# A decoder layer in a three-deep software pipeline: the recurrence of a batch beside the whole next iteration, its feed-forward one iteration later

## The chip, the core and the metric

The kernel runs on one core of one Trainium2 chip. The metric is the device time of one execution in microseconds. All work is inside one launch; the host only lays out the inputs.

## What is computed

Sixteen independent batches of 256 tokens with 512 channels go through one decoder layer: causal self-attention with 16 heads of 32 channels, a recurrence over the tokens that takes the first result as keys and a second input as values, and an attention that has one shared key and value head, chosen for each token by a gate. Each of the three is added to its input and normalised over the channels.

```python
def _wkv(time_decay, time_first, k, v):       # per channel, over 256 tokens
    w, u = -jnp.exp(time_decay), time_first
    def step(carry, kv_t):
        aa, bb, pp = carry
        kt, vt = kv_t
        ww = u + kt
        q = jnp.maximum(pp, ww)
        e1, e2 = jnp.exp(pp - q), jnp.exp(ww - q)
        y_t = (e1 * aa + e2 * vt) / (e1 * bb + e2)
        ...
...
x = _layernorm(x + _L0_attn_ref(x, Wq, bq, Wk, bk, Wv, bv, Wo, bo))
x = _layernorm(x + _L0_xattn_ref(16, 256, 512, time_decay, time_first, x, ctx_2048))
x = _layernorm(x + _L0_ffn_ref(x, W_gate, W_qkv))
```

The feed-forward (`_L0_ffn_ref`) projects x to q, k and v, keeps for each token the k and v of the head that the gate ranks first, and attends causally with all 16 query heads over these.

## The kernel before

**The work of a batch.** Matrix products are made in three passes of a high and a low part (lines 485 to 487). A is the self-attention: six projections (`project_a`, jobs PA_Q, PA_K, PA_V, two each), four groups of four heads, and two output projections (PA_WO). A group has three tiles of scores for the maxima (`scores_sq`, `sq_a`), whose row maxima VectorE takes (`maxima_a`, line 1368); `max_a` turns them (line 547), ScalarE and VectorE split them into high and low rows (`row_hi`, `rows`), and SyncE copies the two rows under the query stack in SBUF (line 332). Only then come the three tiles of scores in the other orientation (`scores_sk`, `sk_a`, lines 563 to 573), their exponentials on ScalarE (line 1031), `values`, a copy, `turn`, and `normalise` on VectorE. F is the feed-forward with the same four groups (`sq_f`, `sk_f`, `values_f`, `turn_f`, `third_residual`), its projections PF_Q, PF_K, PF_V, the gate (`gate_logits`, `gate_transpose`, `gating`), and the choice of key and value (`pick_key`, `pick_value`), after which `key_transpose` (line 733) turns the key.

**The recurrence** is done per block of 128 channels (c = 0 to 3), two blocks at a time. TensorE turns x1 so that channels lie on partitions (`x1_transpose`, line 620, half 0 and half 1, in PSUM bank pw). VectorE runs a scan and a difference (`recurrence_start`, lines 1422 and 1426), ScalarE five passes (`carry_exps`) and one more (`now_exps`), VectorE two scans (`sums`, lines 1437 and 1439), GpSimd the products around them (`weighted`, `products`, `quotient`), VectorE a reciprocal of 256 columns (`divide`, line 1445). TensorE turns the result back (`y_transpose`, line 645), VectorE adds it (`second_residual`), takes statistics (`second_stats`) and normalises (`second_norm`, line 1410). Then `x2_transpose` (line 620 again) feeds the feed-forward, whose q is split by `fq_hi` on ScalarE and `fq_lo` on VectorE (line 1483).

**The order.** Each engine runs one hand-written list of instructions and waits on semaphores; nothing is reordered. `iteration(t)` of TensorE interleaves A of batch t with F of batch b = t - 1, and in its second part projects q, k and v of batch t + 1. The recurrence of batch t starts in that second part (blocks 0 and 1 first, then 2 and 3) and ends in the first part of iteration t + 1: `y_transpose` 0 inside the projection PA_V + 1, `y_transpose` 1 behind `max_a(t, 1)`, `x2_transpose` six groups of instructions later. SyncE's list holds, in this order, the copies of the k stack, two loads of ctx, more of the k and q stacks and then the rows of maxima. Batch 15's recurrence uses a second set of buffers (`far`), and runs beside the second half of F of batch 14; F of batch 15 runs alone at the end. `keep` issues products whose result is not used.

**Memory.** Two buffers hold x (`x_even`, `x_odd`). `w_key` and `w_e1` lie over the last quarter of `k_stack`, so GpSimd puts back two rows of ones after each recurrence (`ones_back`). `picked` lies in `w_val`.

```python
                project_a(t, PA_V + 1, {1: lambda: y_transpose(b, 0), 2: scores})
                sk_a(t, 0, 2)
                max_a(t, 1)
                y_transpose(b, 1)
                ...
                x2_transpose(b, x_by_parity[1 - odd])
```

## Time and profile before

| | |
|---|---|
| median of 3 runs | 1566.29 us (1560.98 to 1566.89) |
| the profiled execution, its own time | 1569.24 us |
| span of its instructions | 1567.4 us |
| TensorE busy | 1419.3 us, 91% |
| VectorE busy | 1124.4 us, 72% |
| ScalarE busy | 640.0 us, 41% |
| GpSimd busy | 412.3 us, 26% |
| iteration 1 | 101 to 202 us |
| iterations 2 to 15 start about every 93 us | 202 to 1415 us |
| ending | about 1477 to 1567 us |

Read the timeline by the last columns: a row with "[1.05 <-DVE neg_max L1368]" is an instruction before which its engine sat idle for 1.05 us, until line 1368 on VectorE released it. A row without brackets followed the one before it. The engines' busy shares are sums over stages; which wait counts is seen at the place where TensorE stands.

### The profile page before, as it was taken

Reading aid. Unit: us, or ns where it says so; the run is one execution under the profiler, and the core shown is the slowest. Engines: PE = TensorE matmul, PEld = TensorE weight load, DVE = VectorE, ACT = ScalarE, POOL = GpSimd, SP = SyncE. Lnnn points to the kernel's source line nnn. Section 1 sums busy time; section 2 is a strip of 40 time slices with the busy share of each in tenths; the row PEclk is TensorE's granted clock in tenths of the full one; section 3 lists DMA queues with packets and bytes.
Section 4 is the critical chain, followed back from the end, with each engine's and each line's share of the span. In section 5 each row is a group of like instructions: output and inputs, shape, how many; then the busy total and the mean of one; then the engine's idle time right before and its main releaser. Section 6 shows DMA issues by size and latency. Waiting matters only on the chain.

```text
span 1567.4 us, 26626 instructions
## 1 busy us (share of the span) xinstructions
PE 1419.3 (91%) x9941; PEld 1123.7 (72%) x9941; DVE 1124.4 (72%) x2260; ACT 640.0 (41%) x1459; POOL 412.3 (26%) x550
## 2 busy tenths in 40 slices
PE   7879999899998989999899999989999998999886
PEld 6667777677777777777777777777777777777564
DVE  4475777868677686776868677786867768677774
ACT  3442533434344253433435344353434425353322
POOL 1350321414122141321414122141412214032130
PEclk9989999999999999999999999999999999999998
DMA  6432232333213233232333313233321323323110
GB/s 192 133 89 68 55 76 57 88 89 79 79 42 82 75 88 89 59 88 52 71 88 79 92 47 74 65 88 89 79 79 42 82 75 89 88 61 80 32 50 20
DMA packets 63199, 119.50 MB, mean 76 GB/s; under 512 B 14304, under 2 KB 32736, under 8 KB 63072
## 3 DMA queue, kind: packets, MB, share of 16 engines
q1 hardware_dynamic: 60400, 112.56, 28.6%
q10 hardware_dynamic: 2672, 5.24, 1.0%
q8 instruction: 80, 1.31, 0.4%
q14 instruction: 47, 0.39, 0.1%
HBM read 32.81 MB, written 8.39 MB: 26 GB/s over the span
## 4 chain that ended last, share of the span: by engine, by line
PE 59%; DVE 26%; ACT 7%; DMA 3%; issue 3%; SPq 1%; POOL 1%; DVEq 0%; ACTq 0%; POOLq 0%
PE pp L485 8%; PE pp L487 7%; PE pp L486 7%; PE po L590 7%; DVE neg_max L1368 5%; DVE w_key L1445 3%; PE po L594 3%; PE sq L531 3%; DVE w_max L1439 2%; PE sq L525 2%; PE pw L485 2%; PE pw L487 2%; PE pw L486 2%; PE sq L510 2%; DMA q_stack<-max_rows 2%
## 5 line engine op out<-in xcount | busy, mean ns | idle before, releaser
L1031 ACT ACTIVATE prob<-sk 128x512 f32<-128x512 f32 x384 | 215.0, 594 | 464.2 <-PE sk L510 463.7
L1368 DVE TENSOR_REDUCE neg_max<-sq 128x2 f32<-128x512 f32 (+1 forms) x384 | 249.7, 677 | 58.0 <-PE sq L510 54.9
L485 PE MATMUL pp<-xt_hi,w_hi 128*128 128x256 f32 x728 | 220.4, 303 | 20.8 <-DVE w_lo L1355 7.3
L487 PE MATMUL pp<-xt_hi,w_lo 128*128 128x256 f32 x728 | 206.3, 283 | 0.0
L486 PE MATMUL pp<-xt_lo,w_hi 128*128 128x256 f32 x728 | 206.3, 283 | 0.0
L485 PEld LDWEIGHTS pp<-xt_hi,w_hi 128*128 128x128 f32 x728 | 139.8, 192 | 32.9 <-issue 11.8
L486 PEld LDWEIGHTS pp<-xt_lo,w_hi 128*128 128x128 f32 x728 | 139.9, 192 | 0.7
L487 PEld LDWEIGHTS pp<-xt_hi,w_lo 128*128 128x128 f32 x728 | 139.6, 192 | 0.0
L1042 ACT ACTIVATE o_ch<-po 128x512 f32<-128x512 f32 x128 | 75.8, 592 | 136.2 <-PE po L594 136.2
L510 PE MATMUL sq<-mask_qk,ident_b 128*128 128x256 bf16 (+1 forms) x384 | 124.7, 325 | 0.0
L485 PE MATMUL pp<-w_hi,xt_hi 128*128 128x512 f32 x252 | 114.2, 453 | 10.7 <-DVE k_lo L1477 10.7
L510 PE MATMUL sk<-mask_kq,ident_b 128*128 128x256 bf16 (+1 forms) x384 | 123.4, 321 | 0.0
L1854 POOL TENSOR_TENSOR w_ev<-w_e,w_val 128x256 f32<-128x256 f32 x62 | 43.6, 704 | 260.8 <-ACT w_e L1089 229.0
L1445 DVE RECIPROCAL w_key<-w_key 128x256 f32<-128x256 f32 x62 | 107.5, 1734 | 0.0
L1820 POOL TENSOR_TENSOR var_eps<-meanvar,eps 128x2 f32<-128x2 f32 x48 | 9.3, 194 | 359.6 <-DVE meanvar L1404 359.6
L487 PE MATMUL pp<-w_hi,xt_lo 128*128 128x512 f32 x252 | 99.6, 395 | 0.0
L486 PE MATMUL pp<-w_lo,xt_hi 128*128 128x512 f32 x252 | 98.9, 392 | 0.0
L563 PE MATMUL sk<-q_stack,kf_stack 98*128 98x512 f32 x192 | 82.1, 467 | 6.9 <-DMA q_stack<-max_rows 3.3
L1373 DVE TENSOR_TENSOR max_rows<-pt,max_rows 8x128 fp32r<-8x128 f32 x128 | 35.3, 276 | 72.5 <-ACT max_rows L1064 70.0
L1839 POOL TENSOR_TENSOR xt_lo<-x_raw,xt_hi 128x1024 fp32r<-128x1024 f32 x15 | 35.6, 2373 | 189.9 <-ACT xt_hi L1102 189.9
L590 PE MATMUL po<-prob,v_f 128*33 128x256 f32 x512 | 80.0, 388 | 3.5 <-ACT prob L1031 2.3
L590 PE MATMUL po<-prob,v_a 128*33 128x256 f32 x512 | 80.7, 393 | 1.1 <-ACT prob L1031 1.1
(237 smaller groups left out, 3537.1 us busy)
## 6 DMA issues: line engine op xcount, KB each, us to landing
q_stack<-q_hi SPq DMA_DIRECT2D x256, 128.0 KB, 2.4
q_stack<-q_lo SPq DMA_DIRECT2D x128, 128.0 KB, 2.4
k_stack<-k_hi SPq DMA_DIRECT2D x128, 128.0 KB, 2.3
x_raw<-in_xT SPq DMA_DIRECT2D x16, 512.0 KB, 3.8
k_stack<-k_lo SPq DMA_DIRECT2D x64, 128.0 KB, 2.3
w_val<-in_ctxT SPq DMA_DIRECT2D x62, 128.0 KB, 2.2
w_raw<-in_weights ACTq DMA_DIRECT2D x4, 1024.0 KB, 6.5
q_stack<-max_rows SPq DMA_DIRECT2D x256, 4.0 KB
```

The source lines that it names most:

```text
L485: T.matmul(out, lh, rh, start=(c == 0), stop=False, skip_group_check=True)
L486: T.matmul(out, lh, rl, start=False, stop=False, skip_group_check=True)
L487: mm = T.matmul(out, ll, rh, start=False, stop=(c == CC - 1), skip_group_check=True)
L510: return T.matmul(out, ident_b[:], tile[:].unsqueeze(1).to_broadcast([P, heads, P]), start=False, stop=True, skip_group_check=True)
L531: T.matmul(out[:, S * k:S * (k + 1)], q_stack[0:3 * HD, h, P:S], key(h, 0, S, 3 * HD), start=(k == 0), stop=False, skip_group_check=True)
L563: T.matmul(out[:].rearrange("p (h q) -> p h q", h=heads), key(h, lo, P, rows), q_stack[0:rows, h:h + heads, q], start=True, stop=False, sk ...
L590: T.matmul(po[VW * j:VW * j + HD + 1, at:at + S], value(0, HG * g + k), prob0[:, k, :], start=True, stop=False, skip_group_check=True)
L594: mm = T.matmul(po[VW * j:VW * j + HD + 1, at + P:at + S], value(1, HG * g + k), prob1[:, k, :], start=False, stop=True, skip_group_check= ...
L1031: A.activation(dst, sk[n % 2][:], ACT.Exp, scale=SCALE).then_inc(s_exp, 1)
L1042: A.activation(o_ch[:].rearrange("p h q -> p (h q)"), po[:], ACT.Copy).then_inc(s_och, 1)
L1368: V.tensor_reduce(dst, src, AX.X, ALU.max, negate=True).then_inc(s_max, 1)
L1445: V.reciprocal(key, key).then_inc(w_rec, 1)
```

## The change

A third stage is put into the pipeline. `iteration(t)` now works on A of batch t, the recurrence of batch r = t - 1, and F of batch b = t - 2. On TensorE `y_transpose(r, 0)` stands behind `values_a(t, 2)`, `y_transpose(r, 1)` ahead of PA_WO, and `x1_transpose(t, 1)` behind the projection PA_V; the order of groups and projections is the old one. Iteration 1 has no F. The ending holds the rest of F of batch 13, F of batch 14 with the recurrence of batch 15 beside it, and F of batch 15; the `keep`s of the ending and the `far` buffers are gone. x has three buffers; `w_key`, `w_e1`, `k_hi`, `k_lo` and `picked` have memory of their own, and `ones_back` is gone. The recurrence and the feed-forward count their use of bank pw in semaphores of their own (`w_*` and `u_*`).

```diff
-W_JOBS, W_X1J, W_YJ, W_X2J, W_GATE, W_GATE_T = 7, 0, 2, 4, 5, 6
+W_JOBS, W_X1J, W_YJ = 4, 0, 2
+U_JOBS, U_X2, U_GATE, U_GATE_T = 3, 0, 1, 2
 CONSTS = 2
...
-        k_stack, far_max, far_e2, far_d, far_e1, far_key, w_key, w_e1 = overlaid(
...
+        k_stack = sb("k_stack", [P, NH, S], f32r)
+        w_key = sb("w_key", [P, HC, S])
+        w_e1 = sb("w_e1", [P, HC, S])
...
-        x_even = sb("x_even", [P, TT, D])
-        x_odd = sb("x_odd", [P, TT, D])
+        x_bufs = [sb(f"x{i}", [P, TT, D]) for i in range(3)]
...
-        picked = w_val[:].rearrange("p c t -> p (c t)").rearrange("p (h d) -> p h d", h=NH)
+        picked_buf = sb("picked", [P, NH, HD])
+        picked = picked_buf[:]
...
-            def iteration(t, odd, last=False):
-
-
-                b = t - 1
+            def iteration(t, last=False):
+
+
+                r, b = t - 1, t - 2
+                f = b >= 0
...
-                project_a(t, PA_V + 1, {1: lambda: y_transpose(b, 0), 2: scores})
+                project_a(t, PA_V + 1, {2: scores})
                 sk_a(t, 0, 2)
                 max_a(t, 1)
-                y_transpose(b, 1)
...
-                x2_transpose(b, x_by_parity[1 - odd])
+                if f:
+                    x2_transpose(b)
                 out_transpose(t, 0)
                 sq_a(t, 2, 2)
                 values_a(t, 1)
-                project_f(b, PF_Q, lambda: max_a(t, 2))
+                if f:
+                    project_f(b, PF_Q, lambda: max_a(t, 2))
+                else:
+                    max_a(t, 2)
                 turn_a(t, 1)
...
                 sq_a(t, 3, 2)
                 values_a(t, 2)
-                project_f(b, PF_K, lambda: max_a(t, 3))
+                y_transpose(r, 0)
+                if f:
+                    project_f(b, PF_K, lambda: max_a(t, 3))
+                else:
+                    max_a(t, 3)
...
+                    pe.wait_ge(dve_f, F_LINKS * b + F_LINK_PICKED + 1)
+                    values_f(b, 0)
+                    max_f(b, 1, a_free, A_JOBS * a_done)
+                y_transpose(r, 1)
                 project_a(t, PA_WO)
-                turn_f(b, 0)
-                project_a(t, PA_WO + 1, lambda: sk_f(b, 1, 0, 1))
-
-                sq_f(b, 2, 0, 1)
-                sk_f(b, 1, 2)
...
+                project_a(t + 1, PA_V, parts)
+                x1_transpose(t, 1)
+                if f:
+                    max_a(t + 1, 0, f_free, F_JOBS * (b + 1))
+                else:
+                    max_a(t + 1, 0)
                 sq_a(t + 1, 1, 0, 1)
 
...
-                second_residual(b, 0, x_b)
...
                 maxima_a(t, 1, 2)
-                if not (isinstance(t, int) and t < 2):
-                    last_third_residual(t - 2, x_t)
+                if b >= 1:
+                    last_third_residual(b - 1, x_of(b - 1))
                 rows_a(t, 1)
-                second_residual(b, 1, x_b)
-                second_stats(chy, b, x_b)
-                chy.close()
                 normalise_a(cha, t, 0)
-                second_norm(b, x_b)
-
+                if t > 1:
+                    sums(r, 2)
                 maxima_a(t, 2, 0, 1)
...
                 rows_a(t, 2)
-                if not (isinstance(t, int) and t < 2):
-                    third_stats(t - 2, x_t)
+                if t > 1:
+                    sums(r, 3)
+                if b >= 1:
+                    third_stats(b - 1, x_of(b - 1))
                 normalise_a(cha, t, 1)
-                gate_out(b)
-                fq_lo(b, 0)
+                if f:
+                    gate_out(b)
+                if t > 1:
+                    divide(r, 2)
+                if f:
...
+                if t > 1:
+                    divide(r, 3)
+                if f:
...
+                    gating(chf, b)
                 rows_a(t, 3)
-                pick_key(chf, b, 0)
+                second_residual(r, 0, x_r)
+                if f:
+                    pick_key(chf, b, 0)
                 normalise_a(cha, t, 2)
...
                 out_lo(t, 3)
-                rows_f(b, 1)
+                if f:
+                    rows_f(b, 1)
+                second_residual(r, 1, x_r)
                 first_residual(t, 0, x_t)
...
+                if f:
+                    maxima_f(b, 3, 0, 1)
                 sums(t, 0)
+                if f:
+                    maxima_f(b, 3, 2)
+                qk_lo(t + 1, PA_K)
+                if f:
+                    rows_f(b, 3)
                 sums(t, 1)
-                maxima_f(b, 3, 2)
-                qk_lo(t + 1, PA_K)
-                rows_f(b, 3)
+                second_stats(chy, r, x_r)
+                chy.close()
+                qk_lo(t + 1, PA_K + 1)
+                if f:
+                    third_residual(chf, b, 2, x_b)
                 divide(t, 0)
+                second_norm(r, x_r)
+                maxima_a(t + 1, 0, 0, 1)
+                maxima_a(t + 1, 0, 2)
+                rows_a(t + 1, 0)
                 recurrence_start(t, 2)
-                qk_lo(t + 1, PA_K + 1)
-                third_residual(chf, b, 2, x_b)
-
                 recurrence_start(t, 3)
                 divide(t, 1)
-                maxima_a(t + 1, 0, 0, 1)
-                sums(t, 2)
-                maxima_a(t + 1, 0, 2)
-                sums(t, 3)
-                rows_a(t + 1, 0)
-                divide(t, 2)
                 maxima_a(t + 1, 1, 0, 1)
-                divide(t, 3)
...
+                    exps_f(b, 3, 0, 1)
+
+                    exps_f(b, 3, 2)
+                    copy_f(b, 3)
+                    row_hi_a(t + 1, 0, f_mrow[NG - 1], 32 * (b + 1))
+                else:
+                    row_hi_a(t + 1, 0, a_mrow[NG - 1], 32 * (t + 1))
+                value_out(t + 1, 0)
                 carry_exps(t, 2)
                 now_exps(t, 2)
-                copy_f(b, 3)
                 carry_exps(t, 3)
                 now_exps(t, 3)
-                row_hi_a(t + 1, 0, f_mrow[NG - 1], 32 * t)
-                value_out(t + 1, 0)
 
             def x2_split_hi(b):
-                for half, s_job, count, bank in ((0, w_job, W_JOBS * b + W_X2J + 1, pw),
...
+            def iteration(t, last=False):
+                r, b = t - 1, t - 2
+                if t > 1:
+                    weighted(r, 2)
+                    weighted(r, 3)
+                    products(r, 2)
+                    products(r, 3)
+                if b >= 1:
+                    inverse_std(b - 1, 2)
+                    third_bias(b - 1)
+                quotient(r, 2)
+                quotient(r, 3)
+                add_bo(t, x_of(t))
+                if not last:
+                    x_split_lo(t + 1)
+                if t == 1:
                     split_lo(W_FV)
-                if prev and not (isinstance(t, int) and t < 2):
-                    inverse_std(t - 2, 2)
-                    third_bias(t - 2)
-                add_bo(t, x_by_parity[odd])
-                x_split_lo(t + 1)
-                if not prev:
-                    split_lo(W_FQ)
                 inverse_std(t, 0)
-                if not prev:
-                    split_lo(W_FK)
+                if last:
+                    inverse_std(r, 1)
+                    return
                 weighted(t, 0)
                 weighted(t, 1)
...
-                b = LAST - 1
+                b = LAST - 2
                 sq_f(b, 2, 2)
-                x1_transpose(LAST, 0, x_by_parity[LAST % 2])
+                x1_transpose(LAST, 0)
+                values_f(b, 1)
                 max_f(b, 2)
-                x1_transpose(LAST, 1, x_by_parity[LAST % 2])
-                values_f(b, 1)
+                x2_transpose(LAST - 1)
                 turn_f(b, 1)
                 sk_f(b, 2, 0, 1)
                 sq_f(b, 3, 0, 1)
-                pe.wait_ge(w_free, W_JOBS * LAST + W_YJ)
-                keep(pw, 9)
+                project_f(LAST - 1, PF_Q)
                 sk_f(b, 2, 2)
-                keep(pw, 10)
                 sq_f(b, 3, 2)
-                keep(pw, 20)
+                values_f(b, 2)
                 max_f(b, 3)
-                values_f(b, 2)
+                project_f(LAST - 1, PF_Q + 1)
                 turn_f(b, 2)
                 sk_f(b, 3, 0, 1)
+                x1_transpose(LAST, 1)
                 sk_f(b, 3, 2)
+                values_f(b, 3)
+                b = LAST - 1
+                gate_logits(b)
+                project_f(b, PF_K)
+                gate_transpose(b)
+                turn_f(b - 1, 3)
+                project_f(b, PF_K + 1)
+                project_f(b, PF_V)
+                key_transpose(b, f_free, F_JOBS * b)
                 y_transpose(LAST, 0)
+                pe.wait_ge(f_free, F_JOBS * b + F_KT + 1)
+                pe.wait_ge(f_max, TILES * b)
+                sq_f(b, 0, 0, 1, 2)
+                project_f(b, PF_V + 1)
+                max_f(b, 0)
+                sq_f(b, 1, 0, 1, 2)
+                pe.wait_ge(f_exp, TILES * b)
+                sk_f(b, 0, 0, 1)
+                max_f(b, 1)
+                sq_f(b, 2, 0, 1)
+                sk_f(b, 0, 2)
+                sq_f(b, 2, 2)
+                pe.wait_ge(dve_f, F_LINKS * b + F_LINK_PICKED + 1)
+                pe.wait_ge(f_norm, NG * b)
+                values_f(b, 0)
+                sk_f(b, 1, 0, 1)
+                turn_f(b, 0)
+                max_f(b, 2)
+                sq_f(b, 3, 0, 1)
...
```

How this moves VectorE's list, at three places of a middle iteration. First, from the maxima of group 0 (batch t + 1) to those of group 1; `w_key<-w_key` is `divide`, `w_max<-decay,pw` with `w_d` is `recurrence_start`, `max_rows` is `rows_a`. Before:

```order
L1368 TENSOR_REDUCE neg_max<-sq 128x2
L1437 SCALAR_TENSOR_TENSOR w_e<-w_e_58,w_e 128x256
L1439 SCALAR_TENSOR_TENSOR w_max<-w_e_58,w_ev 128x256
L1373 TENSOR_TENSOR max_rows<-pt,max_rows 8x128
L1445 RECIPROCAL w_key<-w_key 128x256
L1368 TENSOR_REDUCE neg_max<-sq 128x4
L1368 TENSOR_REDUCE neg_max<-sq 128x2
L1445 RECIPROCAL w_key<-w_key 128x256
L1451 TENSOR_TENSOR x_odd<-pw,x_odd 128x2x256
```

and in the changed kernel, from `rows_a(t + 1, 0)` on:

```order
L1485 TENSOR_TENSOR max_rows<-pt,max_rows 8x128
L1533 SCALAR_TENSOR_TENSOR w_max<-decay,pw 128x256
L1535 MEMSET w_d 128x1
L1537 SCALAR_TENSOR_TENSOR w_d<-pw,decay,w_max 128x255
L1533 SCALAR_TENSOR_TENSOR w_max<-decay,pw 128x256
L1535 MEMSET w_d 128x1
L1537 SCALAR_TENSOR_TENSOR w_d<-pw,decay,w_max 128x255
L1556 RECIPROCAL w_key<-w_key 128x256
L1480 TENSOR_REDUCE neg_max<-sq 128x4
L1480 TENSOR_REDUCE neg_max<-sq 128x2 x2
```

Where one `divide` stood between the rows and the maxima, there are now two `recurrence_start`s and one `divide`; the two `sums` that stood ahead of the rows are gone from here.

Second, around the maxima of group 2: `o_rec`, `o_tok` is `normalise_a(t, 0)`, `xt_lo<-pw,xt_hi` is `x2_split_lo(b, 0)`. Before:

```order
L1392 RECIPROCAL o_rec<-po 128x8
L1393 TENSOR_TENSOR o_tok<-po,o_rec 128x256
L1410 TENSOR_SCALAR x_odd<-x_odd,meanvar,rstd 128x512 x2
L1368 TENSOR_REDUCE neg_max<-sq 128x4
L1368 TENSOR_REDUCE neg_max<-sq 128x2
L1466 TENSOR_TENSOR xt_lo<-pw,xt_hi 128x512
```

and now:

```order
L1504 RECIPROCAL o_rec<-po 128x8
L1505 TENSOR_TENSOR o_tok<-po,o_rec 128x256
L1548 SCALAR_TENSOR_TENSOR w_e<-w_e 128x256
L1550 SCALAR_TENSOR_TENSOR w_max<-w_e,w_ev 128x256
L1480 TENSOR_REDUCE neg_max<-sq 128x4
L1480 TENSOR_REDUCE neg_max<-sq 128x2
L1577 TENSOR_TENSOR xt_lo<-pw,xt_hi 128x512
```

`second_norm` is gone from here, and the two scans of `sums(r, 2)` stand between `normalise_a` and the maxima.

Third, around the first split of the feed-forward's q (`q_lo<-pp,q_hi` is `fq_lo(b, 0)`, `logit_t` is `gate_out`). Before:

```order
L1392 RECIPROCAL o_rec<-po 128x8
L1393 TENSOR_TENSOR o_tok<-po,o_rec 128x256
L1512 COPY logit_t<-pw 16x256
L1483 TENSOR_TENSOR q_lo<-pp,q_hi 128x512
L1368 TENSOR_REDUCE neg_max<-sq 128x4
L1368 TENSOR_REDUCE neg_max<-sq 128x2
```

and now:

```order
L1504 RECIPROCAL o_rec<-po 128x8
L1505 TENSOR_TENSOR o_tok<-po,o_rec 128x256
L1623 COPY logit_t<-pw 16x256
L1556 RECIPROCAL w_key<-w_key 128x256
L1594 TENSOR_TENSOR q_lo<-pp,q_hi 128x512
L1480 TENSOR_REDUCE neg_max<-sq 128x4
L1480 TENSOR_REDUCE neg_max<-sq 128x2
```

A `divide` stands ahead of `fq_lo(b, 0)`; another, `divide(r, 3)`, ahead of `fq_lo(b, 1)`.

## Rows read from the trace of the kernel before

**Rows 1.** The page, part 1: busy time, share of the span and count of each engine.

```profile
PE 1419.3 (91%) x9941; PEld 1123.7 (72%) x9941; DVE 1124.4 (72%) x2260; ACT 640.0 (41%) x1459; POOL 412.3 (26%) x550
```

**Rows 2.** Busy time by engine in stretches (start:end, length, then engines, clock, DMA share, GB/s).

```profile
101.00:202.00 101.00, 92.20 (x622) 73.05 (x621) 69.66 (x132) 37.92 (x88) 29.04 (x34) 0.94 0.26 64
...
1477.00:1509.00 32.00, 23.09 (x175) 15.92 (x175) 28.20 (x53) 13.98 (x35) 17.49 (x22) 0.95 0.03 9
1509.00:1558.00 49.00, 42.57 (x279) 32.74 (x280) 26.31 (x58) 14.31 (x30) 1.24 (x4) 0.97 0.18 44
```

**Rows 3.** Busy time by engine in the four parts of the iteration from 763 to 855.

```profile
763.00:776.00 13.00, 11.27 (x89) 8.82 (x91) 11.49 (x25) 6.28 (x12) 4.41 (x8) 1.00 0.27 62
776.00:799.00 23.00, 23.00 (x165) 19.41 (x162) 14.15 (x37) 8.12 (x19) 2.43 (x5) 1.00 0.34 95
...
829.00:855.00 26.00, 23.07 (x166) 18.04 (x164) 22.08 (x37) 15.98 (x41) 13.20 (x17) 1.00 0.44 103
```

**Rows 4.** Timeline of PE, 757 to 785 us: start, us, line, operation, idle before, releaser.

```profile
759.56 0.27 PE L547 MATMUL pt<-ident,neg_max 128*8 128x128 f32 x1 [1.05 <-DVE neg_max L1368]
...
763.46 0.47 PE L568 MATMUL sk<-q_stack,k_stack 98*128 98x256 f32 x2 [0.70 <-DMA q_stack<-max_rows]
...
764.17 0.48 PE L531 MATMUL sq<-k_stack,q_stack 96*128 96x256 f32 x2
...
767.18 0.27 PE L547 MATMUL pt<-ident,neg_max 128*8 128x128 f32 x1 [0.38 <-DVE neg_max L1368]
...
773.42 0.66 PE L620 MATMUL pw<-ident,x_odd 128*128 128x128 f32 x4 [0.89 <-DVE x_odd L1410]
...
774.48 0.48 PE L531 MATMUL sq<-k_stack,q_stack 96*128 96x256 f32 x2
...
784.27 0.38 PE L485 MATMUL pp<-xt_hi,w_hi 128*128 128x256 f32 x1
```

**Rows 5.** Timeline of DVE, 740 to 750 us: first scan of sums, reciprocal, recurrence start.

```profile
741.09 0.69 DVE L1437 TENSOR_TENSOR_SCAN w_e<-w_e,w_e 128x256 f32<-128x256 f32 x1
...
746.80 1.73 DVE L1445 RECIPROCAL w_key<-w_key 128x256 f32<-128x256 f32 x1
748.46 0.62 DVE L1422 TENSOR_TENSOR_SCAN w_max<-decay,pw 128x256 f32<-128x256 f32 x1
...
749.11 0.48 DVE L1426 SCALAR_TENSOR_TENSOR w_d<-pw,decay,w_max 128x255 f32<-128x255 f32 x1
```

**Rows 6.** Timeline of ACT: first and last of the six passes for block 2.

```profile
753.39 0.41 ACT L1084 ACTIVATE w_e<-w_d 128x256 f32<-128x256 f32 x1
...
755.16 0.49 ACT L1095 ACTIVATE w_d<-w_d,now_high 128x256 f32<-128x256 f32 x1
```

**Rows 7.** Timeline of SyncE, 760 us: the two rows of maxima to the stack.

```profile
760.24 1.98 SPq L332 DMA_DIRECT2D q_stack<-max_rows  x2
```

**Rows 8.** Waits of PE over the whole run: total us, times, longest.

```profile
PE pt L733 <- DVE k_lo L1490: 14.9, 13, 1.4
```

**Rows 9.** Timelines of POOL, DVE and PE, 703 to 708 us: where key_transpose waits.

```profile
703.84 2.54 POOL L1834 TENSOR_TENSOR x_odd<-x_odd,bo_row 128x512 f32<-128x512 f32 x2 [15.27 <-DMA x_odd<-in_x]
...
704.13 1.06 DVE L1545 CAST k<-k_sel 128x64 fp32r<-128x64 f32 x1
...
707.10 0.39 PE L733 MATMUL pt<-ident,k 128*96 128x128 f32 x2 [1.18 <-DVE k_lo L1490]
```

**Rows 10.** Timeline of PE: the first score tile of batches 0, 1 and 2.

```profile
38.34 0.48 PE L568 MATMUL sk<-q_stack,k_stack 98*128 98x256 f32 x2
...
103.64 0.40 PE L568 MATMUL sk<-q_stack,k_stack 98*128 98x256 f32 x2
...
203.03 0.47 PE L568 MATMUL sk<-q_stack,k_stack 98*128 98x256 f32 x2 [0.70 <-DMA q_stack<-max_rows]
```

**Rows 11.** Timeline of PE in the ending: first transposes of x1 and x2 of batch 15.

```profile
1477.57 0.66 PE L620 MATMUL pw<-ident,x_odd 128*128 128x128 f32 x4 [0.88 <-DVE x_odd L1410]
...
1508.95 0.66 PE L620 MATMUL pw<-ident,x_odd 128*128 128x128 f32 x4 [1.50 <-DVE x_odd L1410]
```

700 lines of the change are left out of this document (399 added, 301 removed).

## The prediction

> **What bounds the kernel now.** The first part of the page shows TensorE busy for 1419.3 us, 91% of the span, and VectorE for 1124.4 us, 72% [rows 1]. So the kernel can gain only what TensorE idles, and can lose wherever VectorE is late. Next come the stretches by engine. In the middle of the iteration that starts at 763 us TensorE has no idle time at all (23.00 of 23.00 us, with VectorE at 14.15) [rows 3]. Its gaps lie where VectorE is dense: 11.27 of 13 beside VectorE's 11.49, and 23.07 of 26 beside 22.08 [rows 3]. The granted clock in all three is 1.00, the upper of its two levels (2.4 GHz), so no more comes from the clock there. Last, TensorE's own timeline at the start of an iteration names the waits: 1.05 us for `neg_max` of VectorE, 0.70 for the DMA of `max_rows`, 0.38 for `neg_max` again, 0.89 ahead of the x2 transposes for `second_norm` (L1410) [rows 4]. Together 3.02 us an iteration. That is the pool the change can draw on: 14 x 3.02 = 42 us for iterations 2 to 15.
>
> The sums below are made against the profiled execution (1569.24 us); the median of the runs is 1566.29, 2.95 lower, so I take 2.95 off at the end.
>
> **Part 1: fourteen iterations.** TensorE issues the same products; `y_transpose`, `x1_transpose` and `x2_transpose` only move (four transposes cost 0.66 [rows 4] either way). So its busy time is unchanged and only waits count.
>
> What goes, per iteration:
> - 1.05 at `max_a(t, 0)`: the two `sums` that stood between the maxima of group 0 are gone. A scan takes 0.69 [rows 5], a pair about 1.3. Gone.
> - 0.38 at `max_a(t, 1)`: `divide` (1.73) stood ahead of the last maxima [rows 5]. See below what stands there now.
> - 0.89 ahead of `x2_transpose`: x2 is normalised in the previous iteration. Gone.
> - About 0.3 of a wait on `k_lo` at the iteration's end, since `recurrence_start(t, 2)` no longer stands ahead of it (0.62 + 0.48 [rows 5] against a wait of about that order: I take a third).
> Sum: about 2.6.
>
> What is late next:
> - `sk_a(t, 0)` waits for the copy of the rows, issued at 760.24 and 1.98 long [rows 7]. With the maxima earlier by 1.05, TensorE arrives earlier, but SyncE's list has loads and stack copies ahead of those rows, and I leave it the same time of landing, about 762.8. The wait becomes 1.1 to 1.45 in place of 0.70 (if SyncE is free earlier it stays 0.70). Cost 0.5.
> - `max_a(t, 1)`: VectorE now has two `recurrence_start`s (2 x 1.12 with the memset) and a `divide` (1.66 to the next start) between rows 0 and the maxima of group 1, 3.9 us, where one `divide` of 1.66 stood [rows 5]. `sums(t, 3)` and one more `divide` on the way are gone, so most of it is paid back: a wait of about 0.8 where 0.38 was.
> - `values_a(t, 0)`: ScalarE now has `carry_exps` and `now_exps` of blocks 2 and 3 ahead of the exponentials. One block takes 753.39 to 755.65, 2.26 us [rows 6], two 4.5. Part of it fits the time until the scores are there; 0.6 left.
> - `sk_a(t, 1)` 0.2, from the same shift of the rows.
> - Maxima of group 2: `sums(r, 2)`, 1.3 us, stands ahead of them where `second_norm` stood behind an earlier wait; `sq_a(t, 2)` at 774.48 had no wait [rows 4]. 0.7 where none was.
> - `project_f(b, PF_Q + 1)` starts at 784.27 without a wait [rows 4] and needs `fq_lo(b, 0)`. A `divide` of 1.66 now stands ahead of that: 0.6, the rest goes into VectorE's idle time.
> - `y_transpose(r, 0)`, behind the gating's copies: 0.35.
> New waits: 1.1 to 1.45 (1.2) + 0.8 + 0.6 + 0.2 + 0.7 + 0.6 + 0.35 = about 4.4, against 3.02 + 0.45 for `k_lo` = 3.5 before, of which 0.15 at `k_lo` stays. Net **+0.8 to +1.1; I take +0.8** per iteration, since the small terms overlap. Bounds: if the new places have slack as in the stretch 776 to 799 (VectorE 14.15 of 23), -1.3; if each VectorE insertion shows in full once, +2.0. Fourteen times: **+11 us (-18 to +28)**.
>
> GpSimd has one place in it: it reads and writes x in `add_bo` (2.54 us for two) beside VectorE's cast, which then takes 1.06, and `key_transpose` waits 1.18 [rows 9]; such waits on `k_lo` come to 14.9 us in 13 iterations [rows 8]. The Trainium skill, "SBUF — State Buffer", section "Who interferes with whom", says that such a cast and a GpSimd instruction exclude each other, so that the order of issue decides. By this rule a shift of `add_bo` alone, which the new list of GpSimd makes, could end that wait; the trace agrees in that one of the two is always the longer. I leave the term at 0, and price its end as a rival.
>
> **Part 2: iteration 1 without feed-forward.** From the first score tile of batch 1 to that of batch 2 pass 203.03 - 103.64 = 99.4 us; from batch 0 to batch 1, without a feed-forward, 103.64 - 38.34 = 65.3 us [rows 10]. TensorE's busy time in 101 to 202 is 92.20 [rows 2], so 65 has room for it. I take the second for the first, 34.1 less, and give 0.6 back for the transposes of batch 0's recurrence that iteration 0 doesn't hold: **-33.5**, with the recurrence of batch 0 beside it hidden (-28 to -39). The splits of the feed-forward's weights lie on ScalarE and GpSimd, which are busy for 38 and 29 of 101 us there [rows 2], so I cost them at nothing; without that cover TensorE would wait for them at PF_Q of batch 0.
>
> **Part 3: the ending.** Between the first transposes of x1 and of x2 of batch 15 pass 1508.95 - 1477.57 = 31.4 us [rows 11], for half a feed-forward beside the recurrence, padded with `keep`s. In the new kernel the whole feed-forward of batch 14 must also pass there. Its work is that of the stretch 1509 to 1558: TensorE 42.57, VectorE 26.31; what is there already is TensorE 23.09 (some 9 of it `keep`) and VectorE 28.20 [rows 2]. Added up: TensorE 57, VectorE 54.5. In parallel without loss 57, with the waits seen there (9 of 32 and 6.4 of 49 us idle) 63 to 64; wholly in series 31.4 + 49 = 80. I take 63.5: **+32 (+25 to +49)**.
>
> The third buffer of x, the separate memory of `w_key`, `k_hi` and `picked`, and the lost `ones_back` remove waits of GpSimd and VectorE on readers of those tiles, and none of the waits before TensorE names them [rows 4]: nothing, unless a load of x that can now start earlier delays the rows' copy in SyncE's list, by up to the 1.98 us of one such pair [rows 7], which stays in the upper bound of part 1.
>
> That parts 2 and 3 cancel is not chance: one feed-forward leaves iteration 1, where it was poorly covered, and enters the ending.
>
> Sum: 11 - 33.5 + 32 = +9.5, in the profiled frame 1578.9 us, as a median **1576.0 us**. A change of 0.5% (7.8 us) is about what a measurement of this kernel can tell from none.
>
> **The rivals.**
> - A, faster: the dense stretches relax. VectorE is at 11.49 of 13 and 22.08 of 26 where TensorE waits, at 14.15 of 23 where it doesn't [rows 3]; the change carries 2 `sums`, 2 `divide`s and the normalisation from the first to the second. All 3.02 gone and new waits of half of that: -1.5 x 14 = -21, to 1566.3 - 21 + 4 for faults at the edges = 1549; with nothing new, 1527. For it: the stretch of 23 us has 8.8 us of free VectorE. Against: TensorE has no gap there, neither at 774.48 nor at 784.27 [rows 4], so each instruction put ahead of an evacuation shows at once. 0.20.
> - B, no change: waits only change place (0 x 14) and the edges cancel: 1566. 0.14.
> - D, the cast and `add_bo` no longer meet: 14.9 us less than my sum [rows 8], 1561, or with a little of A beyond the threshold. 0.12, of which 0.02 faster.
> - C, slower still: the ending's VectorE becomes the bound. Its 54.5 us of work go in series with the turns at both ends, +45 rather than +32, and iteration 1, with neither F nor `keep`, loses 5 us by the clock, whose mean in 101 to 202 is 0.94 even with F [rows 2]. The Trainium skill, "TensorE: Matmul & The Clock Gate", part 1, says that a TensorE with too little work falls to half its clock; by that rule the same products of iteration 1 would take up to twice as long while it lasts. Time by the rows: 1576 + 13 + 5 = 1594, 1596 with a little more of the clock. It decides once TensorE waits for VectorE in the ending for over 20 us between the two transposes. 0.12.
> - My forecast, waits up by 0.8 an iteration and edges that cancel: 0.42, of which 0.38 over the threshold and 0.04 within it.
>
> **How the numbers follow.** Faster: A 0.20 + D 0.02 = 0.22. Within 0.5%: B 0.14 + D 0.10 + 0.04 = 0.28. Slower: 0.38 + C 0.12 = 0.50. The range: from 1548, half of A's relief, leaving out some 0.10 below; to 1596, the end of C, with +28 of part 1's bound mostly inside, leaving 0.08 above. The forecast's own range is 1566 to 1588.
>
> **What the profile would show.** Step 1 right: no wait on `neg_max` at `max_a(t, 0)` and none ahead of `x2_transpose`; new ones at `max_a(t, 1)`, at `values_a(t, 0)` behind ScalarE, at PF_Q + 1 behind `q_lo`; iterations of 94 us where they are 93. Wrong: iterations of 92 or less, with TensorE at 93% or more. Step 2: the score tiles of batches 1 and 2 about 65 us apart at a granted clock of 0.9 or more; 75 would break it. Step 3: 63 us between the two transposes in the ending, TensorE's idle time there 6 to 15 us. GpSimd: as many waits of `key_transpose` as in rows 8. The forecast falls if the iterations change by more than 2 us either way, or if parts 2 and 3 differ by over 12 us.

## The result, and the profile after

The changed kernel takes 1623.2 us (median of 4 runs, 1617.6 to 1625.2), the kernel before 1565.0; ratio 1.038, 95% interval 1.036 to 1.041. Forecast were 1576 us and a range up to 1596. The direction was right, the size six times too small.

The first part of the page of the changed kernel, and the row of the clock in forty slices:

```profile
PE 1446.1 (89%) x9858; PEld 1146.9 (71%) x9858; DVE 1101.1 (68%) x2258; ACT 642.2 (40%) x1459; POOL 373.4 (23%) x520
...
PEclk9988899999999999999999999999999999999889
```

The span grew by 56.0 us (1567.4 to 1623.4) [rows 1]. TensorE's busy time grew by 26.8, though its work did not (it issues 83 products fewer, all of them `keep`s); its idle time grew by 29.2. The same product takes longer in some places: a product of L469 with 512 columns takes 0.39 us at 841.00 and 0.63 at 847.50, where the granted clock is 0.50. By stages, busy time of the engines (columns as in [rows 2]):

```profile
275.67:368.69 93.02, 86.33 (x612) 68.77 (x613) 67.55 (x140) 38.07 (x88) 22.10 (x31) 1.00 0.30 75
842.57:940.02 97.45, 87.89 (x613) 70.28 (x613) 69.37 (x140) 40.26 (x93) 22.12 (x31) 0.98 0.30 74
102.69:179.75 77.06, 59.86 (x342) 46.75 (x340) 33.96 (x72) 22.41 (x51) 24.30 (x26) 0.83 0.24 60
...
1480.28:1562.88 82.60, 61.03 (x353) 45.13 (x354) 54.89 (x112) 27.25 (x63) 17.97 (x28) 0.83 0.12 30
1562.88:1623.40 60.52, 44.29 (x293) 32.74 (x291) 30.50 (x71) 17.11 (x34) 2.48 (x8) 0.92 0.17 45
```

The first score tiles of batches 1 and 2 are now at 102.69 and 179.75 us, against 103.64 and 203.03 [rows 10]. The ledger, with the first transposes of x1 and x2 of batch 15 as marks in the ending, as in [rows 11]:

| stretch | before | after | difference | forecast |
|---|---|---|---|---|
| up to the first score tile of batch 1 | 103.64 | 102.69 | -1.0 | 0 |
| iteration 1 | 99.39 | 77.06 | -22.3 | -33.5 |
| iterations 2 to 14 | 13 x 93.26 | 13 x 95.07 | +23.5 | |
| iteration 15 up to the x1 turn | 62.15 | 64.67 | +2.5 | +11 with the row above |
| between the turns of x1 and x2 | 31.38 | 82.60 | +51.2 | +32 |
| the rest | 58.45 | 60.52 | +2.1 | 0 |
| sum | | | +56.0 | +9.5 |

**Inside an iteration.** TensorE's waits at the start of the one at 842.57 (timeline; the idle time and its releaser are in brackets):

```profile
842.57 0.47 PE L550 MATMUL sk<-q_stack,k_stack 98*128 98x256 f32 x2 [0.50 <-DMA q_stack<-max_rows]
...
844.71 0.62 PE L513 MATMUL sq<-k_stack,q_stack 96*128 96x256 f32 x2 [1.18 <-DVE neg_max L1480]
...
849.70 0.63 PE L572 MATMUL po<-prob,v_a 128*33 128x256 f32 x4 [0.67 <-ACT prob L1107]
...
856.22 0.51 PE L513 MATMUL sq<-k_stack,q_stack 96*128 96x256 f32 x2 [0.65 <-DVE neg_max L1480]
...
866.69 0.39 PE L467 MATMUL pp<-xt_hi,w_hi 128*128 128x256 f32 x1 [0.64 <-DVE q_lo L1594]
...
872.02 0.63 PE L641 MATMUL pw<-ident,w_y 128*128 128x128 f32 x4 [0.41 <-DVE logit L1628]
```

The wait of 0.70 for the rows is 0.50, and those of 1.05, 0.38 and 0.89 [rows 4] are gone. In their place stand 1.18 for the maxima of group 1, 0.67 for ScalarE, 0.65 at the maxima of group 2, 0.64 at PF_Q + 1 and 0.41 ahead of y_transpose. VectorE's timeline ahead of the 1.18:

```profile
840.15 0.67 DVE L1533 TENSOR_TENSOR_SCAN w_max<-decay,pw 128x256 f32<-128x256 f32 x1
...
841.25 0.68 DVE L1533 TENSOR_TENSOR_SCAN w_max<-decay,pw 128x256 f32<-128x256 f32 x1
...
842.37 1.74 DVE L1556 RECIPROCAL w_key<-w_key 128x256 f32<-128x256 f32 x1
844.03 1.22 DVE L1480 TENSOR_REDUCE neg_max<-sq 128x4 f32<-128x512 f32 x2
```

Two recurrence starts and a reciprocal of 1.74 stand ahead of the maxima. Averaged over iterations 2 to 14 of the profiled execution, TensorE idles 7.33 us where it idled 6.66: +0.67, against the 0.8 forecast. But it is busy for 87.74 us instead of 86.60, since the granted clock falls right behind these waits (a "dip" below):

```profile
844.00:846.00 2.00, 1.29 (x5) 1.09 (x6) 1.64 (x4) 1.97 (x6) 1.76 (x3) 0.74 0.19 41
846.00:848.00 2.00, 2.00 (x6) 1.52 (x6) 1.26 (x4) 0.78 (x2) 0.25 (x1) 0.50 0.00 0
848.00:850.00 2.00, 1.33 (x11) 0.89 (x11) 0.19 (x1) 1.34 (x3) 0.00 (x0) 0.91 0.00 0
```

In 846 to 848 it is 0.50, the level of 1.2 GHz. An iteration at a mean clock of 1.00 (the first row of the stages, 93.02 us) has 86.33 us of busy time, one with a dip 87.89 and more. Between GpSimd's splits of x, which mark the iterations, 10 of 12 were below 1.00 in the changed kernel, 1 of 13 in the kernel before. So 1.1 of the 1.8 us an iteration is clock. The two iterations without a dip begin with one long wait for the rows and have no 1.18 behind it:

```profile
275.67 0.47 PE L550 MATMUL sk<-q_stack,k_stack 98*128 98x256 f32 x2 [1.93 <-DMA q_stack<-max_rows]
```

### The profile page after: what moved, and what is told of

It is laid out like the page before. It is cut to its first block, busy times and chain, and to the rows that moved or that the text cites. A ratio compares the mean times of both kernels' runs of the same rounds, so it can differ in the third digit from the quotient of the medians.

```text
span 1623.4 us, 26480 instructions
## 1 busy us (share of the span) xinstructions
PE 1446.1 (89%) x9858; PEld 1146.9 (71%) x9858; DVE 1101.1 (68%) x2258; ACT 642.2 (40%) x1459; POOL 373.4 (23%) x520
## 4 chain that ended last, share of the span: by engine, by line
PE 56%; DVE 22%; ACT 11%; DMA 4%; issue 3%; SPq 3%; POOL 0%; ACTq 0%; DVEq 0%; POOLq 0%
PE pp L467 8%; PE pp L469 8%; PE pp L468 8%; PE po L572 5%; PE sq L513 3%; DMA q_stack<-max_rows 3%; DVE neg_max L1480 3%; DVE w_key L1556 3%; ACT prob L1107 2%; PE po L576 2%; PE sq L492 2%; PE sq L507 2%; PE sk L492 2%; PE pw L467 2%; PE po L586 2%
## 5 line engine op out<-in xcount | busy, mean ns | idle before, releaser
L469 PE MATMUL pp<-xt_hi,w_lo 128*128 128x256 f32 x728 | 207.1, 284 | 0.0
L469 PEld LDWEIGHTS pp<-xt_hi,w_lo 128*128 128x128 f32 x728 | 140.5, 193 | 0.0
L467 PE MATMUL pp<-w_hi,xt_hi 128*128 128x512 f32 x256 | 120.8, 472 | 12.0 <-DVE k_lo L1588 12.0
L2030 POOL TENSOR_TENSOR w_y<-w_ev,w_key 128x256 f32<-128x256 f32 x64 | 47.9, 757 | 292.6 <-issue 125.9
L1556 DVE RECIPROCAL w_key<-w_key 128x256 f32<-128x256 f32 x64 | 111.4, 1741 | 0.5
L469 PE MATMUL pp<-w_hi,xt_lo 128*128 128x512 f32 x256 | 107.3, 419 | 0.0
L468 PE MATMUL pp<-w_lo,xt_hi 128*128 128x512 f32 x256 | 107.1, 418 | 0.0
L1504 DVE RECIPROCAL o_rec<-po 128x8 f32<-128x8 f32 x128 | 25.7, 201 | 109.9 <-PE po L586 107.9
L2019 POOL TENSOR_TENSOR w_key<-w_e,w_d 128x256 f32<-128x256 f32 x64 | 46.8, 732 | 221.0 <-DVE w_max L1550 219.9
L513 PE MATMUL sq<-k_stack,q_stack 96*128 96x256 f32 x256 | 72.4, 367 | 22.1 <-DVE neg_max L1480 21.9
```

Source lines behind the costliest of these rows:

```text
L467: T.matmul(out, lh, rh, start=(c == 0), stop=False, skip_group_check=True)
L468: T.matmul(out, lh, rl, start=False, stop=False, skip_group_check=True)
L469: mm = T.matmul(out, ll, rh, start=False, stop=(c == CC - 1), skip_group_check=True)
L513: T.matmul(out[:, S * k:S * (k + 1)], q_stack[0:3 * HD, h, P:S], key(h, 0, S, 3 * HD), start=(k == 0), stop=False, skip_group_check=True)
L1556: V.reciprocal(key, key).then_inc(w_rec, 1)
L2030: G.tensor_tensor(w.y[:, i, :], w.ev[:, i, :], w.key[:, i, :], ALU.mult).then_inc(w_yr, 1)
```

## The experiments

Iteration lengths below are the mean distance of GpSimd's splits of x, over iterations with all three stages, in each run's profiled execution (before 93.26, changed 95.12). The last column counts the iterations whose mean granted clock was below 1.00, in that one execution. One execution's count of dips is not another's: e6 leaves the iterations alone and had 5 of 12 where the changed kernel had 10.

| kernel | us | ratio to before (95%) | iteration | below clock 1.00 |
|---|---|---|---|---|
| e1 divide late | 1620.1 | 1.034 (1.027 to 1.041) | 93.82 | 2 of 12 |
| e2 keep in the gap | 1619.4 | 1.034 (1.029 to 1.038) | 94.44 | 3 of 12 |
| e3 keep at the edges | 1618.4 | 1.035 (1.031 to 1.038) | 95.43 | 9 of 12 |
| e4 ScalarE late | 1619.0 | 1.035 (1.032 to 1.038) | 94.64 | 5 of 12 |
| e5 both late | 1615.5 | 1.033 (1.030 to 1.036) | 94.41 | 6 of 12 |
| e6 ending's order | 1613.7 | 1.031 (1.027 to 1.034) | 94.88 | 5 of 12 |
| e7 before, no keep | 1566.9 | 1.002 (1.001 to 1.004) | 93.30 | 2 of 13 |
| e8 e3, e5 and e6 | 1609.3 | 1.029 (1.026 to 1.032) | 94.94 | 7 of 12 |
| e9 exponentials later | 1596.0 | 1.020 (1.017 to 1.023) | 92.96 | 2 of 12 |
| e10 e9 with the edges | 1589.6 | 1.017 (1.013 to 1.020) | 93.28 | 4 of 12 |
| e11 before, divide early | 1583.4 | 1.013 (1.009 to 1.017) | 94.48 | 6 of 13 |
| e12 e10, middle too | 1618.9 | 1.036 (1.033 to 1.039) | 95.49 | 4 of 12 |
| e14 e12, GpSimd's edit | 1579.1 | 1.009 (1.005 to 1.013) | 92.39 | 1 of 12 |
| e13 e14, two more | 1550.3 | 0.991 (0.988 to 0.994) | 90.38 | 1 of 12 |
| e15 e13 without edges | 1556.6 | 0.995 (0.993 to 0.997) | 90.05 | 1 of 12 |

### The start of an iteration

**e1.** VectorE's list:

```diff
                 recurrence_start(t, 3)
-                divide(t, 1)
                 maxima_a(t + 1, 1, 0, 1)
+                divide(t, 1)
```

> The changed kernel (1623 us) with one edit: in VectorE's list divide(t, 1) stands behind the maxima of group 1, tiles 0 and 1, not ahead of them. In the changed kernel's trace TensorE waits 1.18 us for these maxima soon after the 0.50 us for the rows' copy, and in the 3 us behind that the granted clock is 0.50 (iterations of 95.1 us with it, of 92 to 93 where it stays 1.00). Theory 1 (the two waits close together bring the clock down): the wait goes and with it the dip, -2.8 us in each of some 14 iterations, about 1585 us, mean clock of an iteration 1.00. Theory 2 (the clock falls for the small work at this place, whatever the wait): only the wait goes, -1.2 us each, about 1607 us, clock still 0.98. Theory 3 (the wait only moves to the next thing behind the divide): 1620 to 1625 us.

The 1.18 is gone, and another wait stands two tiles further, for ScalarE:

```profile
736.92 0.47 PE L550 MATMUL sk<-q_stack,k_stack 98*128 98x256 f32 x2 [0.47 <-DMA q_stack<-max_rows]
...
740.70 0.66 PE L555 MATMUL sk<-q_stack,k_stack 98*128 98x128 f32 x4 [1.06 <-ACT prob L1107]
...
742.38 0.63 PE L572 MATMUL po<-prob,v_a 128*33 128x256 f32 x4 [0.67 <-ACT prob L1107]
```

The wait moved (theory 3). The profiled execution was the fastest of four (1605 to 1628); the median is within noise of the changed kernel. That only 2 of its 12 iterations had a dip, with as much idle time in two pieces further apart, may be this execution's alone: its mean granted clock was 0.975, that of the other three 0.963 to 0.971, as in the executions of the changed kernel (0.934 to 0.970).

**e2.** TensorE's list:

```diff
                     sk_a(t, 0, 0, 1)
+                    pe.wait_ge(w_free, W_JOBS * r + W_X1J + 2)
+                    keep(pw, 9)
                     sq_a(t, 1, 2)
```

> The changed kernel with one edit: ahead of sq_a(t, 1, 2), where TensorE waits 1.18 us for VectorE, it issues nine keep products (about 1.05 us of work whose result is not used). VectorE's list is unchanged, so the wait itself stays as long. Theory 1 (idle time brings the clock down): the dip goes, -1.6 us an iteration, about 1601 us. Theory 2 (the small work at this place does): 1623 us or a little more. If the nine products come where TensorE would not have waited they cost up to 1 us an iteration, 1637 us.

The wait of 1.18 fell to 0.20, and in the one profiled execution there were fewer dips (3 of 12). Its iterations were 0.7 us shorter (94.44 for 95.12), 8 us in twelve, but 5 of these were lost again ahead of and behind them, where the lists are the same, and the medians lie within noise of each other. By the time alone it is theory 2; it tells little.

**e4.** ScalarE's list, `carry_exps(t, 3)` and `now_exps(t, 3)` moved across the iteration's end:

```diff
                 exps_a(t, 0, 0, 1)
+                if t > 1:
+                    carry_exps(t - 1, 3)
+                    now_exps(t - 1, 3)
                 value_out(t, 1)
```

> The changed kernel with one edit: on ScalarE carry_exps and now_exps of block 3 stand behind the exponentials of the first two score tiles of the next iteration, not ahead of them. The trace of the changed kernel shows TensorE waiting 0.67 us at values_a(t, 0) for these exponentials in nearly every iteration. Theory 1 (each wait put in by the change costs its length): that wait goes, -0.6 us x 14, about 1615 us, and no more unless the clock's dip is shortened as well (then about 1600). Theory 3 (the wait only moves): sums(t, 3) comes later and the time stays at 1623 us.

Neither wait went: the 1.18 stayed, and so did the 0.67 at `values_a(t, 0)` in nearly all iterations. The moved block was not its cause. In the changed kernel's trace ScalarE has caught up by then and stands waiting for TensorE's scores, and in the kernel before `y_transpose` stood in the gap that is now bare (the first row is ScalarE's in the changed kernel, the second TensorE's in the kernel before):

```profile
848.96 0.60 ACT L1107 ACTIVATE prob<-sk 128x512 f32<-128x512 f32 x1 [0.20 <-PE sk L492]
```

```profile
767.29 0.62 PE L645 MATMUL pw<-ident,w_y 128*128 128x128 f32 x4
```

The median, 1619.0, lies between the theories and within noise of the changed kernel.

**e5.** e1 and e4 together.

> The changed kernel (1623 us) with both edits at the start of an iteration: divide(t, 1) behind the maxima on VectorE, and block 3 of carry_exps and now_exps behind the first exponentials on ScalarE. Alone, the first took the 1.18 us wait away and left a new one of 1.06 us for ScalarE's exponentials two tiles later; the second alone left the 1.18. Theory A (VectorE's and ScalarE's share of the recurrence are two covers over the same gap): with both gone neither wait stands, 1.2 to 1.8 us less an iteration, and the clock stays at 1.00 in most iterations, so 92 us an iteration and 1583 to 1590 us in all. Theory B (a third one, the copy of the rows or the maxima of group 2, takes their place): 93.3 us or more an iteration, 1605 to 1620 us.

Theory B. The two waits became one:

```profile
745.04 0.47 PE L550 MATMUL sk<-q_stack,k_stack 98*128 98x256 f32 x2 [0.47 <-DMA q_stack<-max_rows]
...
750.37 0.63 PE L572 MATMUL po<-prob,v_a 128*33 128x256 f32 x4 [1.71 <-ACT prob L1107]
```

and behind it the clock fell again (windows of 3 us from 747):

```profile
747.00:750.00 3.00, 1.66 (x10) 1.04 (x8) 2.54 (x5) 2.97 (x9) 2.08 (x3) 1.00 0.02 3
750.00:753.00 3.00, 2.63 (x20) 1.89 (x20) 0.28 (x1) 0.96 (x3) 0.11 (x1) 0.71 0.01 3
753.00:756.00 3.00, 3.00 (x14) 2.63 (x14) 0.00 (x0) 0.75 (x2) 0.00 (x0) 0.50 0.58 131
```

**e9.** As e5, but ScalarE's piece stands behind `exps_a(t, 0, 2)` and `row_hi_a(t, 1)`.

> The changed kernel (1623 us) with divide(t, 1) behind the maxima and block 3 of the recurrence's exponentials behind the third score tile's exponentials and the rows of group 1, so that neither VectorE nor ScalarE has a piece of the recurrence in front of anything TensorE needs in the first 8 us of an iteration. With block 3 one step earlier, TensorE waited 1.72 us for ScalarE at values_a(t, 0) instead of 1.18 and 0.67. Theory 1 (these waits can be taken away, and the clock's dip follows them): 0.5 us of waits in that place, clock 1.00 in nearly every iteration, 91.5 to 92 us an iteration, 1575 to 1590 us. Theory B (the wait goes on to the next place, maxima or copies): 93 us an iteration, 1600 to 1615 us.

Now the 1.18 goes and no other wait comes for it: 27 us off the changed kernel, of which its page shows 16.2 as TensorE's busy time (1446.1 to 1429.9). Two iterations of it:

```profile
643.23:735.51 92.28, 86.42 (x612) 68.93 (x613) 68.17 (x140) 38.85 (x90) 22.15 (x31) 1.00 0.29 76
735.51:827.87 92.36, 86.44 (x612) 68.93 (x613) 68.33 (x140) 38.75 (x90) 22.16 (x31) 1.00 0.30 76
```

It ends between the two theories (92.96 us an iteration): the waits in that place are 0.5 for the rows and 0.5 for ScalarE, those of the middle stayed.

**e11**, the mirror, in the kernel before:

```diff
                 divide(t, 2)
+                divide(t, 3)
                 maxima_a(t + 1, 1, 0, 1)
-                divide(t, 3)
```

> The kernel before with one edit: divide(t, 3) stands ahead of the maxima of group 1, tiles 0 and 1, beside divide(t, 2), so that VectorE comes to these maxima 1.7 us later, as it does in the changed kernel. Theory 1 (a wait at this place close behind the 0.70 us for the rows costs its length and also brings the clock down): 1.2 to 1.7 us of new wait in each of 14 iterations, 17 to 24 us, and a granted clock of 0.98 in most iterations, 1.6 us each, together 1595 to 1610 us. Theory 2 (the clock's dips come from something else in the changed kernel): clock 1.00 as before, 1582 to 1590 us. Theory 3 (slack behind it takes the wait up): 1565 to 1570 us.

TensorE at the start of an iteration:

```profile
773.10 0.50 PE L531 MATMUL sq<-k_stack,q_stack 96*128 96x256 f32 x2 [0.97 <-DVE neg_max L1368]
...
776.52 0.63 PE L590 MATMUL po<-prob,v_a 128*33 128x256 f32 x4 [0.23 <-ACT prob L1031]
```

0.97 and 0.23 stand where 0.38 stood [rows 4]. The median is 19 us longer (interval 14 to 26), which is theory 2's time; the clock is on theory 1's side, since 6 of 13 iterations were below 1.00 where 1 was, and the mean granted clock of its four executions was 0.980 to 0.986 against 0.986 to 0.993 of the kernel before. In the profiled execution iterations 2 to 14 took 15.8 us more, 4.9 of it idle time and 10.9 TensorE's busy time. So it is theory 1's mechanism, with a smaller wait and fewer dips than I had priced: one reciprocal in the wrong place of the old kernel makes the same kind of loss. That the dips come from idle time close together is what e2, e9 and e11 point to; it is not shown. How much idle it takes was not tried. e5 shows dips behind some of its 1.72 waits and not behind others, and e6, whose iterations have the list of the changed kernel, has 0.49 and 1.18 at 649.84, 1126.69 and 1318.21 without a dip.

### The edges

**e3.** keeps in six places of iteration 1 (72 products) and six of the ending (124), for instance

```diff
                     turn_f(b - 1, 3)
+                pe.wait_ge(f_exp, TILES * b)
+                keep(sk[0], 30)
                 project_f(b, PF_K + 1)
```

> The changed kernel with keep products put into the long waits of iteration 1 (six places, 72 products) and of the ending (six places, 124 products), nothing else. In the changed kernel's trace the granted clock is 0.83 in both stretches. Theory 1 (a good part of their length is the low clock): iteration 1 from 77.1 to about 69 us, the ending's 82.6 to about 75, together some 15 us, 1608 us. Theory 2 (these stretches are bound by VectorE, ScalarE and the copies, and TensorE's clock hardly matters there): both keep their length within 3 us, 1620 to 1626 us.

The clock came up to 0.92 and 0.96 in the two stretches, from 0.83:

```profile
101.00:175.40 74.40, 62.34 (x419) 49.06 (x417) 37.12 (x74) 23.72 (x55) 26.62 (x29) 0.92 0.26 65
1479.00:1559.00 80.00, 70.06 (x501) 52.41 (x501) 56.25 (x116) 28.84 (x67) 17.98 (x28) 0.96 0.12 31
```

Iteration 1 took 72.5 us where it took 77.1, and the stretch between the turns of x1 and x2 77.0 (1479.20 to 1556.24) where it took 82.6: 10 us of the 15 of theory 1, so each lies between the theories. The median moved by 5 only, and in the profile the other iterations were 0.3 us longer each. The clock is a part of both: some 5 us of the 11 by which iteration 1 missed its forecast, and some 6 us of the 19 by which the ending did. At a clock of 0.96 the ending's stretch is still 46 us longer than before.

**e6.** VectorE's list in the ending, with `y_transpose(LAST, 1)` and `x2_transpose(LAST)` earlier on TensorE; its core:

```diff
                 gate_out(r)
+                gate_copy(r)
                 third_residual(chf, b, 3, x_of(b))
-                sums(LAST, 2)
                 third_stats(b, x_of(b))
                 chf = Chain(dve, dve_f, F_LINKS, r)
-                gating(chf, r)
-                sums(LAST, 3)
+                gating(chf, r, False)
                 pick_key(chf, r, 0)
+                sums(LAST, 2)
                 pick_key(chf, r, 1)
-                divide(LAST, 2)
+                sums(LAST, 3)
```

> The changed kernel with another order in the ending alone. VectorE: the gate's logits are copied out ahead of the third residual and the statistics, the picks ahead of sums 2 and 3 of batch 15, the divides behind the first maxima, the second norm of batch 15 beside the maxima of group 3; TensorE turns the recurrence's second half back and x2 of batch 15 earlier. The changed kernel's ending has single waits of 4.1, 3.8, 3.3 and 1.9 us for VectorE, 21 us of idle time in 82.6. Theory A (the ending's excess over my 63.5 us is the order of VectorE's list): 8 to 12 us less, about 1612 us. Theory B (feed-forward 14 has nothing beside it that could fill TensorE, so the waits come back at other places): no more than 4 us less, 1619 us or more.

From the x1 turn to the end 136.0 us, 7 less: the single waits of 4.1 and 3.8 became 1.7, 2.4 and 0.9. The median is 9.5 us below the changed kernel's, theory A's size, though only 7 of the 11 us between the two profiled executions lie in the ending; the other 46 us over the kernel before stay.

**e7.** The kernel before without five of the six keeps of its ending (73 of 83 products).

> The kernel before, without the five keeps (73 products, some 9 us of TensorE) of its ending; nothing else. Theory A (there they hold the clock while TensorE waits for the recurrence of batch 15): the 31.4 us between the turns of x1 and x2 stay within 2 us, the products behind them begin at a granted clock of 0.5, and the whole is 1 to 5 us longer, 1566 to 1570 us. Theory B (they are in TensorE's way): 1 to 4 us shorter.

Theory A: the median is 2.9 us longer (0.1 to 0.4%), the stretch between the turns took 32.4 us (1476.81 to 1509.24), and the first products behind its last wait, of 4.12 us, ran at a clock of 0.50. TensorE was busy there for 18.3 us and idle for 14.2; this is the stretch without its padding.

**e8, e10.** e8 is e3's keeps of iteration 1 with e5, e6 and keeps in four places of the ending; e10 the same with e9 in e5's place.

> The changed kernel with all of it: both edits at the start of an iteration, keeps in the long waits of iteration 1, the other order in the ending with keeps in three waits. If the parts add up as single runs show (iteration 1 with keeps -5 to -7 us, the ending's order -4 to -12, the start of the iterations 0 to -35): 1580 to 1610 us. To come level with the kernel before (1565 us) it would need 92 us an iteration and an ending below 70 us; I expect it still to be slower.

> The same start of the iterations, with the keeps in iteration 1, and the other order and the keeps in the ending. The ending and iteration 1 gave 10 to 13 us together. Theory 1: 1565 to 1580 us, level with the kernel before at best. Theory B: 1595 to 1607 us.

e8 took 1609.3 us, at the upper end of its range. e10 took 1589.6, outside both of its ranges and nearer theory B.

### The middle of an iteration

**e12.** e10, with VectorE's list in the first part rearranged: `sums(r, 2)` behind `rows_a(t, 2)`, `sums(r, 3)` behind `gate_out`, `divide(r, 2)` behind `out_lo(t, 1)`, the gate's copy ahead of `fq_lo(b, 1)`, `divide(r, 3)` behind `rows_a(t, 3)`.

> The kernel e10_all_later (1589.6 us) with the rest of the recurrence's pieces moved behind what TensorE waits for: sums(r, 2) and sums(r, 3) behind the maxima and rows of group 2, divide(r, 2) behind fq_lo(b, 0), divide(r, 3) behind the rows of group 3, and the copy of the gate's turned logits ahead of fq_lo(b, 1). In the trace of e9_exps_later these pieces cost TensorE 0.65 us at the maxima of group 2, 0.34 at the projection behind fq_lo and 0.41 ahead of y_transpose. Theory 1 (the waits go): -1.4 us an iteration, about 91 us each, 1568 to 1574 us in all. Theory B (they turn up again at the key's turn or the products behind it): 1585 to 1592 us. Either way the stretch behind the last x_split stays 40 to 45 us longer than in the kernel before, so that a deeper pipeline needs iterations of 90.5 us or less to win.

A miss: 29 us slower. The waits of TensorE in the iteration at 748:

```profile
773.05 0.63 PE L572 MATMUL po<-prob,v_a 128*33 128x256 f32 x4 [1.64 <-ACT prob L1125]
...
775.63 0.63 PE L641 MATMUL pw<-ident,w_y 128*128 128x128 f32 x4 [1.09 <-DVE logit L1646]
...
780.86 0.50 PE L467 MATMUL pw<-w_hi,xt_hi 128*128 128x512 f32 x1 [1.13 <-DVE x L1581]
```

ScalarE stands before `third_norm`, with the exponentials (L1125) that TensorE needs behind it:

```profile
770.91 1.52 ACT L1233 ACTIVATE x<-x,token_ln,rstd 128x512 f32<-128x512 f32 x2 [3.78 <-POOL token_ln L2017]
772.33 0.57 ACT L1125 ACTIVATE prob<-sk 128x512 f32<-128x512 f32 x1
```

and what it waits for stands on GpSimd behind the six products of blocks 2 and 3, which wait for the `sums` that I had moved back:

```profile
763.76 0.74 POOL L2047 TENSOR_TENSOR w_key<-w_e,w_d 128x256 f32<-128x256 f32 x1 [9.06 <-DVE w_max L1569]
...
767.27 0.72 POOL L2047 TENSOR_TENSOR w_key<-w_e,w_d 128x256 f32<-128x256 f32 x1 [1.27 <-DVE w_max L1569]
...
768.77 0.73 POOL L2050 TENSOR_TENSOR w_ev<-w_max,w_ev 128x256 f32<-128x256 f32 x1
...
770.67 0.20 POOL L2017 TENSOR_TENSOR token_ln<-token_ln,rstd 128x2 f32<-128x2 f32 x1
```

**e14.** The edit in GpSimd's list alone. **e13.** That, `divide(r, 3)` moved behind the copy of the turned key, and `sums(r, 3)` ahead of `gate_out` (an edit of VectorE's list that its expectation leaves out).

```diff
                     products(r, 2)
-                    products(r, 3)
                 if b >= 1:
                     inverse_std(b - 1, 2)
                     third_bias(b - 1)
+                if t > 1:
+                    products(r, 3)
```

> The kernel e12_mid_too (1618.9 us) with two edits: in GpSimd's list the inverse deviation and third_bias of the batch ahead of products(r, 3), not behind it; in VectorE's list divide(r, 3) behind the copy of the turned key, not ahead of second_residual(r, 0). In the trace of e12_mid_too ScalarE stands 3.78 us ahead of third_norm for GpSimd's last small product, which stands behind six products of the recurrence, and TensorE then waits 1.64 us for the exponentials, 1.09 for the copied logits and 1.13 for second_residual. Theory 1 (that one place in GpSimd's list is the whole reason why e12_mid_too is 29 us above e10_all_later): the three waits go, iterations of about 91 us, 1568 to 1578 us. Theory 2 (moving the sums back is itself too late for what follows): 1590 us or more.

> The kernel e12_mid_too (1618.9 us) with the edit in GpSimd's list alone: inverse deviation and third_bias ahead of products(r, 3). divide(r, 3) stays ahead of second_residual(r, 0), sums(r, 3) behind gate_out. e13_bias_first, which has all three edits, took 1550.3. Theory 1 (the one place in GpSimd's list was the cause, by 3.8 us on ScalarE): TensorE's waits of 1.64 and 1.09 us go, the 1.13 for second_residual behind the divide stays: 1565 to 1572 us. Theory 2 (both places needed to go): 1590 us or more.

The GpSimd edit brings 40 us, the other two, not tried apart, 29. So the one place in GpSimd's list is the larger cause and not the whole: e14 at 1579.1 lies above its theory 1 (1565 to 1572), and e13 at 1550.3 below its own (1568 to 1578). In e14 TensorE still waits in 14 places for `second_residual`, which stood behind the divide; in e13 in none:

```profile
PE pw L467 <- DVE x L1581: 16.0, 14, 1.2
```

And e13 is faster than the kernel before, by 0.6 to 1.2%. One iteration and the stretch between the turns:

```profile
719.94:809.40 89.46, 85.98 (x612) 68.94 (x613) 66.88 (x140) 38.66 (x90) 22.79 (x31) 1.00 0.32 78
1413.92:1488.13 74.21, 61.10 (x393) 45.29 (x394) 53.65 (x110) 26.17 (x62) 17.74 (x28) 0.91 0.13 34
```

89.46 us, of which TensorE is busy 85.98. Even the waits of `key_transpose` [rows 8, 9] are gone in the iterations. VectorE's second cast of the key now comes 33 us into the iteration and takes 0.20, and GpSimd's `add_bo`, behind `quotient(r, 3)`, 38 us into it:

```profile
753.19 0.20 DVE L1679 CAST k<-k_sel 128x64 fp32r<-128x64 f32 x1
```

```profile
757.46 0.73 POOL L2057 TENSOR_TENSOR w_y<-w_ev,w_key 128x256 f32<-128x256 f32 x1 [11.35 <-issue]
758.15 2.52 POOL L2021 TENSOR_TENSOR x<-x,bo_row 128x512 f32<-128x512 f32 x2
```

(The first fence is VectorE's timeline, the second GpSimd's.) In the changed kernel the same two met, at 880.63 and 880.18; the cast took 0.90 and the addition behind it (`k<-k_sel,k`) 1.20, where it takes 0.19 in e13.

**e15.** e13 without the keeps and the ending's order.

> The changed kernel with all edits of e13_bias_first in the iterations and none in iteration 1's waits and the ending: no keeps, the ending's order as it was. The single runs put keeps and the ending's order at 5 and 10 us. Theory 1 (they add up): 10 to 14 us above e13_bias_first, 1560 to 1565 us, about level with the kernel before. Theory 2 (they are worth nothing once the iterations are even): 1550 to 1554 us.

1556.6 us, between the theories: 6 above e13, less than half of what the edges' parts had given singly, and 0.3 to 0.7% faster than the kernel before. The third stage with even lists pays for its longer ending without any edit of the ending. Whether the kernel before would gain as much from a new order of its own lists was not tried, so that the gain is the third stage's and not the order's is not shown.

## Why the prediction was wrong

The step that failed most is in part 3: that feed-forward 14 and the recurrence of batch 15 pass the ending in parallel, in 63.5 us. They took 82.6, about as long as one behind the other. By the prediction's own sign it falls, since parts 2 and 3 differ by 29 us and not by less than 12; its other sign, iterations within 2 us, held (+1.8).

- **"Net +0.8 per iteration"**: most waits were right one by one (0.65 and 0.64 where 0.7 and 0.6 were forecast, 0.67 for 0.6, 0.41 for 0.35, 1.18 for 0.8 one instruction earlier than I had put it; 0.50 for 1.2 was not) and in sum (+0.67). The 0.67 at `values_a` was luck: priced was ScalarE's share of the recurrence, seen is the place that `y_transpose` left (e4), and 0.52 of it stays in e9, where that share is out of the way. What failed is the sentence that TensorE's "busy time is unchanged and only waits count". I read the clock of 1.00 in [rows 3] as a given of the stretch and not as something that the spacing of its waits upholds; in the profiled execution the dips added 1.1 us to each iteration and the term came to 26 instead of 11, within its bound of +28. That the spacing does it is argued, as said at e11.
- **"I take the second for the first: -33.5"**: the stretch of batch 0 has keeps in it, and its clock was 0.95; iteration 1 has neither. TensorE's busy time is 59.86 against 52.13, its idle time 17.2 against 13.2, and the keeps of e3 brought back 4.6 of the 11.2 us by which the term missed. The new waits are those for which the feed-forward had been the cover:

```profile
PE sk L550 <- DMA q_stack<-max_rows: 4.6, 3, 2.2
PE pp L467 <- DVE k_lo L1588: 3.8, 2, 1.9
PE pp L467 <- DVE q_lo L1588: 2.5, 2, 1.8
```

  The one pair of evacuations, 1.8 to 1.9 us, shows in full between projections that share a bank, and so does the copy of the rows.
- **"In parallel without loss 57, with the waits seen there 63 to 64"**, the largest error, 19 of 46 us. TensorE's busy time came to 61.0, with the lower clock; VectorE's to 54.9, as forecast (54.5). But TensorE idles 21.6 us, not 6.5. The sentence names two idle times, 9 of 32 and 6.4 of 49 us, and adds only the second to 57; with both it would have been 72. And the 9 is what the `keep`s had left over: without them e7 idles 14.2 us in that stretch. e7's stretch and the one from x2's turn to 1558 (49.05 us, TensorE busy for 42.6), one behind the other, make 81.5 us, 60.9 busy and 20.6 idle; measured are 82.6, 61.0 and 21.6. It came out as if neither had filled a wait of the other; that is a sum of rows, no run tests it. The largest waits:

```profile
PE sq L513 <- DVE neg_max L1480: 6.3, 3, 3.8
PE pw L467 <- DVE logit L1628: 4.1, 1, 4.1
PE pw L602 <- DVE x L1522: 3.6, 2, 2.7
PE po L572 <- DVE o_tok L1505: 3.3, 1, 3.3
```

  In these lists TensorE has nothing ready meanwhile. Part of it is their order: with e6's the stretch takes 72.8 us, and the end comes 7 us earlier. Rival C is the nearest: +51 for its +45, and iteration 1 at a clock of 0.83 is its other half, though 11 us and not 5. Its rule, over 20 us of waits for VectorE between the turns, is just missed, with 18.8 of the 21.6, and its reason is not what is seen: VectorE is busy for 54.9 of the 82.6 us, so not the amount of its work bounds the stretch but where its pieces stand. I gave it 0.12. The rule of the Trainium skill, "TensorE: Matmul & The Clock Gate", part 1, that a TensorE with too little work is clocked down, agrees with the 0.83 of both edges and, what I had not applied, with the dips in the iterations.
- **Rivals A and D** fell for the kernel as it stood. `key_transpose` still waits for `k_lo` 12 times, 12.9 us. (That one of the two that meet is always the longer, as the prediction says, holds only where they do meet: the cast at 797.36 in the kernel before takes 0.20 and `add_bo` begins behind it.) But e13 and e15 show that A named the right place: VectorE's free time in the middle stretch can take the recurrence's pieces, to 3.2 us less an iteration than before. What I had not seen is that a piece's place costs more than its length, in either direction, and through engines two steps away.
- That parts 2 and 3 "cancel" was the step that hid the risk: part 3 was sized by work, part 2 by a stretch with keeps in it, and both failed the same way, -22 and +51.

## What to carry to other kernels

A deeper pipeline trades cover: a stage that leaves a stretch takes its filler along, and the fill and drain must be priced by the waits that then stand bare, not by busy time. In a kernel of hand-ordered lists, price every piece ahead of an evacuation with the engines behind it: one place in GpSimd's list was worth 40 us here, one reciprocal of VectorE's 19. Where TensorE is above 90% busy, look at the granted clock right behind each pair of waits before calling its busy time fixed.

## What the runs showed of the hardware

In the changed kernel's trace the granted clock fell to 0.50 in ten of twelve iterations, each time for 3.4 us, worth 1.6 to 1.8 us. It fell behind idle pieces of 0.50 and 1.18 us (842 to 845), of 1.08 and 0.52, and of 1.76 in one; behind one of 1.93 (at 275.67) it did not. In e5 it fell for 6.8 us behind 1.71 (751 to 758), and behind the same wait in other iterations not at all. The same list of instructions had 10 of 12 such iterations in one execution (changed kernel) and 5 of 12 in another (e6). VectorE's cast of 0.20 us took 0.90 beside GpSimd's `add_bo` (880.63 in the changed kernel), and 0.20 again where the two stood 5 us apart (e13).
